# Cross attention on one core: four score banks, three single maxima banks, row maxima reduced bank by bank

## The reference, cut to what matters

```python
ci = rms_norm(hidden_states, ln_post_cross_w)
cq = heads(ci @ cq_w, NH, CHD)                 # 16 heads of 16 columns
ckv = encoder_outputs @ ckv_w                  # 1601 keys
ck, cv = jnp.split(ckv, 2, axis=-1)
ck, cv = (heads(ck, NH, CHD), heads(cv, NH, CHD))
cctx = sdpa(cq, ck, cv, causal=False)          # softmax over the keys, then the weighted values
cctx = cctx.transpose(0, 2, 1, 3).reshape(b, l, CC)
hidden_states = hidden_states + cctx @ cdense_w
```

## Time and profile before

| what | us |
|---|---|
| median of 3 runs | 2149.52 (2146.91 to 2151.99) |
| the profiled execution | 2146.5, of it span 2144.4 |
| main loop of the cross attention, from its first fills to its last values | about 1082 to 1645 of the span |
| VectorE reductions L2233 | 480, 992 ns each |
| ScalarE exponentials L2167 | 832, 595 ns each |

### The profile page before, as it was taken

The page is one execution under the profiler, slowest core; times in us unless marked ns, Lnnn a source line. Parts: engine busy times, 40 slices in busy tenths (PEclk is TensorE's granted clock), DMA queues, the critical chain, the costliest instruction groups (busy, mean ns, idle before and its releaser), DMA issues. The chain is left out here.

```text
span 2144.4 us, 32835 instructions
## 1 busy us (share of the span) xinstructions
PE 1995.5 (93%) x12637; PEld 1333.4 (62%) x12654; DVE 1527.6 (71%) x2138; ACT 1008.1 (47%) x1748; POOL 509.6 (24%) x496
## 2 busy tenths in 40 slices
PE   7899998899979997888879999999999899999998
PEld 5788775777745554676634444444435677777786
DVE  5676786788847775656589999999963575766564
ACT  1232413555425554444348888888885132221111
POOL 0321321244401223332101313223132212221211
PEclk9999999899969999999979999999999999999999
DMA  4222021433477653686545344453500433334332
GB/s 141 72 101 81 20 73 50 153 124 124 128 184 179 176 132 109 225 254 208 153 108 107 69 90 86 77 100 67 106 17 17 123 95 109 97 109 112 92 92 65
DMA packets 176330, 237.20 MB, mean 111 GB/s; under 512 B 26730, under 2 KB 106862, under 8 KB 174218
## 3 DMA queue, kind: packets, MB, share of 16 engines
q1 hardware_dynamic: 165904, 222.86, 38.5%
q0 software_dynamic: 7856, 10.90, 1.8%
q10 hardware_dynamic: 2400, 1.12, 0.2%
HBM read 169.80 MB, written 62.91 MB: 109 GB/s over the span
## 5 line engine op out<-in xcount | busy, mean ns | idle before, releaser
L2167 ACT ACTIVATE pT_x<-ps 128x512 f32<-128x512 f32 (+1 forms) x832 | 451.7, 595 | 93.6 <-PE ps L2323 67.4
L2233 DVE TENSOR_REDUCE quarters<-ps 128x2 f32<-128x804 f32 x480 | 454.2, 992 | 45.2 <-PE ps L2273 43.8
L2338 PE MATMUL ps<-pT_x,vx_ring 128*17 128x256 f32 (+1 forms) x3328 | 261.4, 387 | 0.0
L1329 DVE TENSOR_REDUCE row_max_s<-ps 128x1 f32<-128x384 f32 (+3 forms) x176 | 109.5, 633 | 65.6 <-PE ps L1361 64.8
L1301 ACT ACTIVATE pT_s<-ps 128x512 f32<-128x512 f32 (+1 forms) x176 | 96.1, 559 | 113.6 <-PE ps L1386 111.6
L114 PE MATMUL ps<-mi_l,w_hi 128*128 128x512 f32 (+1 forms) x352 | 140.1, 398 | 0.0
L2512 POOL TENSOR_TENSOR sg<-sg,keep_all 128x512 f32<-128x512 f32 (+1 forms) x44 | 70.0, 1591 | 289.3 <-ACT sg L2486 289.3
L113 PE MATMUL ps<-mi_h,w_lo 128*128 128x512 f32 (+1 forms) x352 | 138.6, 394 | 0.0
L112 PE MATMUL ps<-mi_h,w_hi 128*128 128x512 f32 (+1 forms) x352 | 138.3, 393 | 0.0
L2338 PEld LDWEIGHTS ps<-pT_x,vx_ring 128*17 128x17 f32 (+1 forms) x3328 | 55.6, 95 | 110.6 <-issue 73.3
L108 DVE TENSOR_TENSOR w_lo<-w_raw,w_hi 128x512 fp32r<-128x512 f32 (+1 forms) x161 | 117.4, 729 | 5.5
(11 more groups left out here) (382 smaller groups left out, 4939.6 us busy)
## 6 DMA issues: line engine op xcount, KB each, us to landing
qkv_l<-self_q_by_part SPq DMA_DIRECT2D x48, 256.0 KB, 4.3
qkv_h<-self_k_by_part SPq DMA_DIRECT2D x48, 256.0 KB, 6.5
w_raw<-L_xattn_l_gate SPq DMA_DIRECT2D x40, 256.0 KB, 2.9
w_raw<-L_xattn_l_up SPq DMA_DIRECT2D x40, 256.0 KB, 2.9
w_raw<-L_xattn_l_down SPq DMA_DIRECT2D x40, 256.0 KB, 2.9
kx_first<-cross_k_by_part SPq DMA_DIRECT2D x36, 200.2 KB, 7.1
cross_v_by_group<-v_aug SPq DMA_DIRECT2D x16, 442.0 KB, 3.9
vx_ring<-cross_v_by_group SPq DMA_DIRECT2D x16, 442.0 KB, 9.8
```

What stands on the lines that cost most here:

```text
L1329: nc.vector.tensor_reduce(out=row_max[:, g % 2, j:j + heads, q], in_=heads_of(bank, heads, (q + 1) * P), axis=AX.X, op=ALU.max)\
L2167: nc.scalar.activation(pT[0:kn, u % 3, j, :], ps[0:kn, 5 + v % 3, :], ACT.Exp, scale=SCALE)\
L2233: nc.vector.tensor_reduce(out=quarters[:, g % 2, pair, :, q, quarter], in_=ps[:, at:at + 2, 0:MAXW], axis=AX.X, op=ALU.max)\
L2338: last = nc.tensor.matmul(ps[j * HD:j * HD + CHD + 1, 4, queries], v_r[0:kn, g % RING, kt, j, :], pT[0:kn, u % 3, j, queries], start=kt == ...
```

## The change

Banks are dealt out anew. Scores use four banks, 3, 5, 6 and 7, in turn; values stay in bank 4; the side work uses banks 0, 1 and 2 one at a time. A unit "max" now takes two places in the numbering, any other unit one. VectorE reduces the two banks of a unit in two instructions, and each gives its bank back when it is done. TensorE waits, before it fills both banks of a unit, until the bank of place n-2 was read: that is the first bank of the unit before, if that unit was a max too. The first matmul of a unit also signals on its own. A pair of scores waits for one exponential fewer. The sums of the first norm after the loop go to bank 3 in place of bank 1.

```diff
-            banked = [o for o in order if o[0] in ("max", "turn", "dense")]
-            place = {o: n for n, o in enumerate(banked)}
+            place, end = {}, 0
+            for o in order:
+                if o[0] != "flip":
+                    place[o] = end
+                    end += 2 if o[0] == "max" else 1
+            SIDE, SCORES, VALUES = 3, [3, 5, 6, 7], 4
...
-                                nc.scalar.activation(pT[0:kn, u % 3, j, :], ps[0:kn, 5 + v % 3, :], ACT.Exp, scale=SCALE)\
+                                nc.scalar.activation(pT[0:kn, u % 3, j, :], ps[0:kn, SCORES[v % 4], :], ACT.Exp, scale=SCALE)\
...
-                                    nc.vector.tensor_reduce(out=quarters[:, g % 2, pair, :, q, quarter],
-                                                            in_=ps[:, at:at + 2, 0:MAXW], axis=AX.X, op=ALU.max)\
+                                    nc.vector.tensor_reduce(out=quarters[:, g % 2, pair, 0, q, quarter:quarter + 1],
+                                                            in_=ps[:, at, 0:MAXW], axis=AX.X, op=ALU.max)\
+                                        .then_inc(s["s_used"], 1)
+                                    dve.wait_ge(s["s_fill"], n + 2)
+                                    nc.vector.tensor_reduce(out=quarters[:, g % 2, pair, 1, q, quarter:quarter + 1],
+                                                            in_=ps[:, (n + 1) % SIDE, 0:MAXW], axis=AX.X, op=ALU.max)\
                                         .then_inc(s["s_used"], 1)
...
-                            at = 2 * (n % 2)
-                            if n >= 2:
-                                pe.wait_ge(s["s_used"], n - 1)
+                            at = n % SIDE
+                            if o[0] == "max" and n >= SIDE - 1:
+                                pe.wait_ge(s["s_used"], n + 2 - SIDE)
+                            elif n >= SIDE:
+                                pe.wait_ge(s["s_used"], n + 1 - SIDE)
...
+                                    if par == 0:
+                                        last.then_inc(s["s_fill"], 1)
...
-                            pe.wait_ge(s["s_used"], place["max", NG - 1, UNITS - 1] + 1)
+                            pe.wait_ge(s["s_exp"], 4 * NG * KT)
...
-                            if v >= 2:
-                                pe.wait_ge(s["s_exp"], v - 1)
+                            if v >= 4:
+                                pe.wait_ge(s["s_exp"], v - 2)
```

More of the change, by code:

```diff
@@ L2148, in keep_sums @@
                                 act.wait_ge(s["s_at"], g - 1)
-                            nc.scalar.activation(osb[:, g % 2, :], ps[:, 4, :], ACT.Copy).then_inc(s["s_ob"], 1)
+                            nc.scalar.activation(osb[:, g % 2, :], ps[:, VALUES, :], ACT.Copy).then_inc(s["s_ob"], 1)
                         def high(n):
@@ L2177, in _ @@
                         act.wait_ge(s["s_tot"], 1)
-                        nc.scalar.activation(rs_first, ps[:, 1, :], ACT.Ln, bias=eps_col[:, 0:1], scale=1.0 / D).then_inc(s["s_root"], 1)
+                        nc.scalar.activation(rs_first, ps[:, SCORES[0], :], ACT.Ln, bias=eps_col[:, 0:1], scale=1.0 / D).then_inc(s["s_root"], 1)
                         act.wait_ge(s["s_root"], 1)
@@ L2249, in _ @@
                                 if o[0] == "max" and o[2] == UNITS - 1:
-                                    dve.wait_ge(s["s_used"], n + 1)
+                                    dve.wait_ge(s["s_used"], n + 2)
                                     find_row_max(g)
@@ L2272, in fill @@
                                     rows = slice(par * STEP, par * STEP + SHIFT)
-                                    last = nc.tensor.matmul(ps[:, at + par, 0:MAXW], q_slots[g % RING][rows, pair, q * P:(q + 1) * P],
+                                    last = nc.tensor.matmul(ps[:, (n + par) % SIDE, 0:MAXW], q_slots[g % RING][rows, pair, q * P:(q + 1) * P],
                                                             k_slots[g % RING][rows, pair, k0:k0 + MAXW], start=True, stop=True)
+                                    if par == 0:
+                                        last.then_inc(s["s_fill"], 1)
                             elif o[0] == "turn":
@@ L2283, in dense_part @@
                             n, b, j = place[o], o[1], o[2]
-                            at, cols_j = 2 * (n % 2), slice(j * P, (j + 1) * P)
+                            at, cols_j = n % SIDE, slice(j * P, (j + 1) * P)
                             if k == 0:
-                                pe.wait_ge(s["s_used"], n - 1)
+                                pe.wait_ge(s["s_used"], n + 1 - SIDE)
                                 pe.wait_ge(s["s_cl"], ET)
@@ L2294, in first_chunks @@
                         def first_chunks():
-                            pe.wait_ge(s["s_used"], place["max", NG - 1, UNITS - 1] + 1)
+                            pe.wait_ge(s["s_exp"], 4 * NG * KT)
                             for k in range(DT):
                                 pe.wait_ge(s["s_sq"], k + 1)
-                                last = nc.tensor.matmul(ps[:, 1, :], ones[:, :], squares[:, k, :], start=k == 0, stop=k == DT - 1)
+                                last = nc.tensor.matmul(ps[:, SCORES[0], :], ones[:, :], squares[:, k, :], start=k == 0, stop=k == DT - 1)
                             last.then_inc(s["s_tot"], 1)
@@ L2318, in scores @@
                             v = 4 * u + 2 * pair
-                            if v >= 2:
-                                pe.wait_ge(s["s_exp"], v - 1)
+                            if v >= 4:
+                                pe.wait_ge(s["s_exp"], v - 2)
                             for par in range(2):
                                 rows = slice(par * STEP, par * STEP + SHIFT + 1)
-                                nc.tensor.matmul(ps[0:kn, 5 + (v + par) % 3, :], k_slots[g % RING][rows, pair, k0:k0 + kn],
+                                nc.tensor.matmul(ps[0:kn, SCORES[(v + par) % 4], :], k_slots[g % RING][rows, pair, k0:k0 + kn],
                                                  q_slots[g % RING][rows, pair, :], start=True, stop=True).then_inc(s["s_sc"], 1)
@@ L2337, in values @@
                             for j in range(4):
-                                last = nc.tensor.matmul(ps[j * HD:j * HD + CHD + 1, 4, queries], v_r[0:kn, g % RING, kt, j, :],
+                                last = nc.tensor.matmul(ps[j * HD:j * HD + CHD + 1, VALUES, queries], v_r[0:kn, g % RING, kt, j, :],
                                                         pT[0:kn, u % 3, j, queries], start=kt == 0 and part == 0,
```

## The result

The changed kernel takes **2218.84 us** (median, 2218.19 to 2221.26) against 2148.22 us for the kernel before, measured beside it: a ratio of 1.0328, 95% interval 1.0316 to 1.0341. That is 70.6 us slower; 2224 had been forecast, 2200 to 2252 as the range. The profiled execution has a span of 2217.4 us.

The account below looks back on a forecast made before the run. The prediction took the loop to be bound by TensorE's stream plus its second fills. Its terms 74 + 5 - 3 - 1 = +75 us on a median of 2149.5 gave 2224 us, range 2200 to 2252.

Parts of the forecast that it names:

- Part 1, the gate: In the loop, a second fill waits 1.12 us, until the first bank of the unit before is reduced: +74 us.
- Single halves: Half steps of the loop with one fill; the next fill comes at 1.18 us anyway, so they were to cost nothing.
- doubles: Half steps with two fills, 7 a group; each was to cost 1.12 in place of 0.39 us, 0.73 us more.
- Part 2, the extra reductions at nothing: VectorE's two reductions for one in the loop: nothing, hidden by the gate; without that cover 32 us.
- Part 3, the fills ahead of the loop: The fills before the first scores, at half clock, come 1.37 us apart in place of 0.90: +5 us.
- Part 4, the fourth score bank: Scores wait less for exponentials: -3 us in the steps after the last fill, -1 us in the loop.
- The milder loss: Rival: the fourth bank frees the loop's single halves, which shrink to 1.12 us, giving 2201 us; chance 0.08.
- Faster: Rival: split reductions remove the stalls at the loop's second fills and score waits fall, -9 us, 2140 us; chance 0.05.
- The clock: Rival: TensorE's idle time in doubles brings half clock in the loop, 100 us more, 2324 us; chance 0.07.

Follow-up runs that it names:

- half_first: The changed kernel with the first reduction of each unit looking only at 201 of its bank's 402 columns; 2191.61 us, ratio 1.0203 to the kernel before.
- half_second: The changed kernel with the second reduction of each unit looking only at 201 of its bank's 402 columns; 2218.76 us, ratio 1.0330 to the kernel before.
- ring4: The changed kernel, split reductions kept, with four banks for the side work and three for scores; 2152.91 us, ratio 1.0028 to the kernel before.
- three_scores: The changed kernel with scores back on three banks and the old wait, one bank unused; 2226.64 us, ratio 1.0372 to the kernel before.
- late_bank: The kernel before with bank 1 as a fourth score bank from step 191 on, when no maxima are left; 2144.72 us, ratio 0.9980.

## Why the prediction was right

**Part 1, the gate, held to the hundredth where it could be read.** Second fills start 1.11 to 1.12 us after the first (1.12 forecast); the first reduction takes 0.58 us (0.58). half_first moved the gate by the length of the reduction, half_second didn't move it. Single halves kept 1.16 to 1.18 us. A group grew by 38.31 - 33.60 = 4.7 us, where 7 x 0.73 = 5.1 had been worked out; over 14.6 groups of fills 69 against 74. The trace shows where the rest went: doubles cost 0.72 us each, single halves are 0.01 us shorter (0.2 a group), and the half before a turn takes 1.06 us in place of 1.16.

One reading was wrong, and the sum escaped it because it took the measured distance. The prediction calls the 0.36 us of six doubles the distance "where nothing holds it", and says that a second fill was held only once in seven. These fills were held too, by the unit two before. The reduction of 1208.53 ends at 1209.53, and the second fill of the double at 1209.22 starts at 1209.58, when its weight load names VectorE:

```profile
1209.58 0.19 PEld L2273 LDWEIGHTS ps<-dense_h,dense_l 63*128 63x128 f32 x2 [0.18 <-DVE quarters L2233]
```

So 0.36 us is a gate as well: 0.49 + 1.00 + 0.05 us after the fill before, less the 1.18 us between those two. ring4 moved it to 0.42 us by the 0.055 us that its two reductions take longer.

**Part 2, the extra reductions at nothing, was right, and its cover is the gate.** ring4 took the cover away and showed 6 us. The forecast's price without cover, 32 us, was too high: it counted VectorE's added 0.06 to 0.07 us at every unit, while ring4 pays them only at the doubles.

**Part 3, the fills ahead of the loop:** 1.37 us apart, as forecast.

**Part 4, the fourth score bank, was sized too small, in the loop above all.** -3 and -1 were forecast. three_scores puts it at 7.8 to 9.3 us by the medians; its profile puts 4.6 us behind the last fills, of which 1 is clock, and 2 in the loop. The rest isn't located. late_bank and the kernel before, both with a spell of half clock there, differ by 74.1 - 71.1 = 3.0 us between the third copy of sums from the end and the last, so the tail's -3 was right. In the loop the waits from which the -1 was taken didn't fall (2.7 us before, 3.0 in the changed kernel). Single halves became 0.01 us shorter there with the fourth bank (1.17 us on average against 1.18 in three_scores); what shortens them is not shown.

**The sum.** Parts 1 and 3 alone give 74 + 5 = 79 us, and three_scores, the kernel with just these, lay 2226.64 - 2146.72 = 79.9 us above the kernel before beside it. That this comes so close to 79 is in part luck: the profiles, cut from the first fill to the last copy of sums, show 76.2 us for three_scores and 69.8 for the changed kernel. So the forecast of +75 lay 4 to 5 us above what was measured for two reasons of about the same size: parts 1 and 3 came out some 3 us smaller, and the fourth bank gave some 6 us in place of 4.

**The rivals.** The milder loss, single halves shrinking to 1.12, didn't come. Faster: the next fill would have needed the bank free 0.36 us after its fill, and the reduction didn't begin before 0.48. The clock: from 1130 on it stayed at 1.00 in the changed kernel's loop, although TensorE stood still for 0.66 us at every double:

```profile
1130.00:1640.00 510.00, 447.14 (x4336) 165.71 (x4334) 458.30 (x892) 386.40 (x711) 113.34 (x190) 1.00 0.40 75
```

It was not far off: half_second, with the same stalls, fell to half clock once in its loop, as shown at the end.

## What to carry to other kernels

Splitting an instruction that frees two buffers frees the first of them sooner, but this helps the next fill only if it doesn't have to wait for a later unit in exchange. What counts is the time from a fill to the release that the next fill waits for (in the ring of three 0.49 + 0.58 + 0.05 us after the fill directly before), compared with the closest distance at which the producer asks (here 0.36 us or less, not the average of 1.0). Look for the place where requests come closest together, and count how many of them a ring takes without a wait. Before a scarce buffer is moved from one ring to another, see whether it is idle in some phase: the last 17 steps had banks to spare and gave 3.5 us without a loss elsewhere.

## What the runs showed of the hardware that was not expected

One idle spell of TensorE can cost its clock or not. Before the last turn it stood still for 1.44 us in the kernel before and in late_bank, and for 1.49 us in the changed kernel, in ring4 and in three_scores; half clock followed in all of them but the changed kernel, as its rows above show. In half_first and half_second it stood still there for 1.28 and 1.29 us, and full clock stayed. The same chain in ring4 kept full speed for one more half step before it fell (halves of 1.18, 1.45 and then 1.71 us):

```profile
1596.46 0.50 PE L2337 MATMUL ps<-dense_l,kx_last 64*128 64x512 f32 x2
...
1597.64 0.54 PE L2337 MATMUL ps<-dense_l,kx_last 64*128 64x512 f32 x2
...
1599.09 0.79 PE L2337 MATMUL ps<-dense_l,kx_last 64*128 64x512 f32 x2
```

It is worth 1.0 us with three score banks (three_scores) and 1597.26 - 1593.84 - 2 x 0.98 = 1.5 us with four (late_bank), which a comparison of two profiles can mistake for an effect.

A shorter idle spell did it too. In half_second TensorE stood still for 0.98 us within the first group, and half clock followed for 6.8 us; at the same place the changed kernel stood still for 1.18 us and kept full speed. Two rows of half_second (the columns of the second are those of a group above), and then one of the changed kernel:

```profile
1131.19 0.70 PE L2283 MATMUL ps<-kx_last,dense_l 63*128 63x402 f32 x2 [0.98 <-DVE quarters L2237]
```

```profile
1131.00:1137.80 6.80, 6.61 (x38) 2.33 (x38) 2.38 (x7) 3.26 (x6) 1.08 (x2) 0.50 0.01 2
```

```profile
1131.91 0.46 PE L2283 MATMUL ps<-kx_last,dense_l 63*128 63x402 f32 x2 [1.18 <-DVE quarters L2237]
```

A reduction from PSUM has a record of 0.56 to 0.58 us for 402 columns, but in ring4's row of them each starts 0.485 us after the one before it: the records overlap. Twice the single record, 1.15 us, would have overstated VectorE's work by nearly a fifth.
